# Cross attention with sixteen heads: the last key's share as a spread matmul and a VectorE product added to the diagonal blocks

## The reference, cut to what matters

```python
# x: 32 sequences of 32 queries, 512 wide; ctx_1024: 32 sequences of 257 keys, 512 wide
Q = (x_q @ W_Q + b_Q).reshape(B, L, H, dk).transpose(0, 2, 1, 3)
K = (x_k @ W_K + b_K).reshape(B, S, H, dk).transpose(0, 2, 1, 3)
V = (x_v @ W_V + b_V).reshape(B, S, H, dk).transpose(0, 2, 1, 3)
scores = jnp.einsum('bhld,bhsd->bhls', Q, K) / jnp.sqrt(jnp.float32(dk))
attn = jax.nn.softmax(scores, axis=-1)
ctx = jnp.einsum('bhls,bhsd->bhld', attn, V)
ctx = ctx.transpose(0, 2, 1, 3).reshape(B, L, H * dk)
out = ctx @ W_O + b_O
```

## Time and profile before

| what | us |
|---|---|
| median of 3 runs | 2437.06 |
| lowest and highest of them | 2435.38 and 2444.72 |
| the profiled execution | 2455.45 |
| its span in the trace | 2453.7 |
| set-up block of `cross_heads`, from its first matmul | about 971 to 1003 |
| its main block | about 1003 to 1611 |

### The profile page before, as it was taken

How to read it: one execution, slowest core, us unless ns; L and a number is a source line. 1 busy time by engine, 2 the same in 40 slices (tenths; PEclk the granted TensorE clock), 3 DMA queues, 4 the chain that set the end, 5 groups by cost and what they waited for, 6 DMA issues and landing times. The chain is left out here.

```text
span 2453.7 us, 39271 instructions
## 1 busy us (share of the span) xinstructions
PE 2102.0 (86%) x14020; PEld 1784.9 (73%) x14020; DVE 1126.3 (46%) x2057; ACT 898.0 (37%) x1479; POOL 926.3 (38%) x638
## 2 busy tenths in 40 slices
PE   6895888837999973999999999977665999999994
PEld 5543777637999962688888888865544999999993
DVE  4245463765555537222223322348754445544543
ACT  2112121214666642233333333223222555555551
POOL 2002312105777763222222222213212666666654
PEclk9996999957999986999999999968876999999997
DMA  3482000016888874011100100010003566656653
GB/s 124 178 312 108 18 19 33 1 35 238 277 278 279 280 230 175 23 33 27 35 26 26 31 31 26 18 48 5 22 22 129 198 217 213 211 198 217 214 194 124
DMA packets 102452, 299.03 MB, mean 122 GB/s; under 512 B 10912, under 2 KB 27936, under 8 KB 102336
## 3 DMA queue, kind: packets, MB, share of 16 engines
q1 hardware_dynamic: 76928, 232.88, 28.3%
q0 software_dynamic: 11840, 38.81, 5.1%
q10 hardware_dynamic: 13600, 26.22, 2.9%
HBM read 265.10 MB, written 32.77 MB: 121 GB/s over the span
## 5 line engine op out<-in xcount | busy, mean ns | idle before, releaser
L134 PE MATMUL banks<-ra 128*128 128x256 f32 (+3 forms) x3004 | 983.6, 328 | 65.9 <-DVE x L1040 24.3
L135 PE MATMUL banks<-ra 128*128 128x256 f32 (+3 forms) x3004 | 968.9, 323 | 0.1
L136 PE MATMUL banks<-ra 128*128 128x256 f32 (+3 forms) x3004 | 965.1, 321 | 3.4 <-issue 3.1
L134 PEld LDWEIGHTS banks<-ra 128*128 128x128 f32 (+1 forms) x3004 | 578.9, 193 | 131.8 <-issue 50.4
L136 PEld LDWEIGHTS banks<-ra 128*128 128x128 f32 (+1 forms) x3004 | 578.7, 193 | 45.2 <-issue 1.3
L135 PEld LDWEIGHTS banks<-ra 128*128 128x128 f32 (+1 forms) x3004 | 580.0, 193 | 39.0 <-issue 3.1
L1475 POOL TENSOR_TENSOR ra<-fa,ra 128x1024 fp32r<-128x1024 f32 x187 | 446.3, 2387 | 237.3 <-ACT ra L1508 236.3
L1508 ACT ACTIVATE ra<-fa 128x1536 fp32r<-128x1536 f32 x190 | 281.5, 1482 | 85.4 <-DMA fa<-in_L_units 68.2
L1592 DVE TENSOR_TENSOR ra<-fa,ra 128x256 fp32r<-128x256 f32 x190 | 162.1, 853 | 92.0 <-ACT ra L1532 91.5
L332 POOL TENSOR_TENSOR ra<-fa,ra 128x2048 fp32r<-128x2048 f32 (+2 forms) x22 | 85.7, 3905 | 285.3 <-ACT ra L326 278.6
L1567 DVE TENSOR_TENSOR ra<-fa,ra 128x512 fp32r<-128x512 f32 x190 | 133.6, 703 | 115.8 <-ACT ra L1508 109.0
(11 more groups left out here) (219 smaller groups left out, 2505.3 us busy)
## 6 DMA issues: line engine op xcount, KB each, us to landing
fa<-in_L_units SPq DMA_DIRECT2D x190, 768.0 KB, 4.5
fa<-in_ctxT SPq DMA_DIRECT2D x64, 514.0 KB, 4.1
ea_y_scratch<-fa ACTq DMA_DIRECT2D x35, 512.0 KB
fa<-in_ctx SPq DMA_DIRECT2D x32, 512.0 KB, 5.3
eb_y_scratch<-fa ACTq DMA_DIRECT2D x15, 512.0 KB, 3.6
fa<-in_L_attn_w_qkvT SPq DMA_DIRECT2D x6, 1024.0 KB, 7.3
normed_scratch<-na SPq DMA_DIRECT2D x16, 256.0 KB, 2.1
x<-in_x SPq DMA_DIRECT2D x1, 2048.0 KB, 8.6
```

What stands on the lines that cost most here:

```text
L134: pe.matmul(psum, lh, rh, start=first, stop=False)
L135: pe.matmul(psum, lh, rl, start=False, stop=False)
L136: return pe.matmul(psum, ll, rh, start=False, stop=last)
```

## The change

The last key's share of the output leaves `p_v`. Its probabilities are spread over the 32 values of a head by one matmul, and multiplied by the last key's values.

- Set-up: the job `None` computes the values of the last key the other way round, with `W_V` as the weights (still in `staging[1]` in full fp32) and the 32 columns of `lastT` moving, in 16 matmuls. VectorE adds the bias in one instruction, and makes `diag` in another. The store to DRAM and its two waits are gone. GpSimd makes `spread`, 128 by 128 with ones in blocks of 32 by 32, and no longer clears `vl`.
- POOL, each sequence: a product of 128 elements, `diag` times the last column of `pr` (`p_last[u]`), behind the normalisation.
- PE, each sequence: the ninth transpose becomes a matmul of 128 by 128 by 128, `spread` by `p_last[u]`, into bank 0. The four matmuls over four rows are gone from `p_v`.
- DVE, each sequence: a new product (`o_last`) of bank 0 and the last key's values between the copy of the second transposed half and `tops`; the four copies into `ot` become four additions with `o_last`.
- ACT loses the small copy of line 1856, SP the load of line 1787 and the wait before it.

```diff
                         if job is None:
...
-                            for c in range(DC):
-                                for part in range(2):
-                                    ins = pe.matmul(banks[0:B, 7, :], lastT[:, c, :], wv[part][:, c, :].bitcast(F32),
-                                                    start=c + part == 0, stop=c == DC - 1 and part == 1)
+                            for i in range(DC):
+                                for c in range(DC):
+                                    ins = pe.matmul(banks[:, 7, i * B:(i + 1) * B], staging[1][:, c, i * P:(i + 1) * P],
+                                                    lastT[:, c, :], start=c == 0, stop=c == DC - 1)
...
                         pool.tensor_tensor(pr[u][:, :, 0:S], pr[u][:, :, 0:S],
                                            rinv[:, u, :].unsqueeze(2).to_broadcast([P, DC, S]),
                                            ALU.mult).then_inc(s_pn, 1)
+                        eng.wait_ge(s_pn, m + 1)
+
+                        eng.sem_inc(s_norm, 1)
+                        shape = [P, DC, NQ]
+                        pool.tensor_tensor(p_last[u], diag.unsqueeze(1).to_broadcast(shape),
+                                           pr[u][:, :, S - 1:S].to_broadcast(shape), ALU.mult).then_inc(s_pl, 1)
...
-                        eng.wait_ge(s_t, 3 * n + 3)
-                        act.activation(pt[0:DC, 2, 0:P], banks[0:DC, 0, 0:P], ACT.Copy).then_inc(s_ta, 1)
...
                         dve.tensor_copy(pt[:, 1, :], banks[:, T1, :]).then_inc(s_td, 1)
+
+                        eng.wait_ge(s_bc, n + 1)
+                        dve.tensor_tensor(o_last, banks[:, 0, 0:P].rearrange("p (c q) -> p c q", c=DC),
+                                          v_last[:, :, bass.ds(n, 1)].to_broadcast([P, DC, NQ]), ALU.mult).then_inc(s_ol1, 1)
                         if after:
                             tops(n + 1, (j + 1) % 2)
                             sums(n + 1, (j + 1) % 2)
 
                         eng.wait_ge(s_pv, n + 1 + LEAD)
+                        eng.wait_ge(s_ol1, n + 2)
...
-                            ins = dve.tensor_copy(ot[rows, :, NQ * j:NQ * j + NQ], o[rows, :, rows])
+                            ins = dve.tensor_tensor(ot[rows, :, NQ * j:NQ * j + NQ], o[rows, :, rows], o_last[rows], ALU.add)
...
-                            eng.wait_ge(s_ta, 2 * m)
+                            eng.wait_ge(s_ol1, m)
...
-                        pe.transpose(banks[0:DC, 0, 0:P], pr[u][:, :, S - 1], ident[:]).then_inc(s_t, 1)
+                        eng.wait_ge(s_pl, n + 1)
+                        pe.matmul(banks[:, 0, 0:P], spread, p_last[u].rearrange("p c q -> p (c q)"), start=True,
+                                  stop=True).then_inc(s_bc, 1)
...
-                        eng.wait_ge(s_vld[u], 32 * g + 16 * (j // 2 + 1))
                         for c in range(DC):
                             cols = slice(c * P, (c + 1) * P)
                             for k in range(2):
-                                pe.matmul(banks[:, T1, cols], v[u][:, k, cols], pt[:, k, cols], start=k == 0, stop=False)
-                            ins = pe.matmul(banks[:, T1, cols], vlast[u][0:DC, cols], pt[0:DC, 2, 0:P], start=False,
-                                            stop=True)
+                                ins = pe.matmul(banks[:, T1, cols], v[u][:, k, cols], pt[:, k, cols], start=k == 0,
+                                                stop=k == 1)
```

More of the change, by code:

```diff
@@ L1667, in cross_heads @@
             qt, bvb, bob = f.take(DC, T), f.take(D), f.take(D)
-            bqc, bkc = f.take(DC), f.take(DC)
+            bqc, bkc, bvc = f.take(DC), f.take(DC), f.take(DC)
+            own, spread, diag, v_last = f.take(4), f.take(P), f.take(NQ), f.take(DC, B)
             qg = [f.take(DC, NQ) for _ in range(2)]
@@ L1672, in cross_heads @@
             staging = [f.take(DC, D) for _ in range(3)]
-            lastT, vl = f.take(DC, B), f.take(DC, D)
+            lastT = f.take(DC, B)
             wk, wv, wo = ((r.take(DC, D), r.take(DC, D)) for _ in range(3))
@@ L1681, in cross_heads @@
             layer_norm("nd", ahead=((load, high, low), (0, 1, 2), (0,)))
-            s_b, s_mm, s_out, s_vl = sem("xb_biases"), sem("xb_product"), sem("xb_taken"), sem("xb_last_v")
-            s_zero = sem("xb_zeros")
+            s_b, s_mm, s_out = sem("xb_biases"), sem("xb_product"), sem("xb_taken")
+            s_zero, s_own = sem("xb_zeros"), sem("xb_own_heads")
             s_ld = [sem(f"xb_ctx{u}") for u in range(2)]
@@ L1696, in _ @@
                                      (bob, d["L1_xattn_b_O"].partition_broadcast(P)),
+                                     (bvc, d["L1_xattn_b_Vc"]),
                                      (lastT, d["ctxLastT"])):
@@ L1703, in _ @@
                         eng.dma_start(stg[u][:, :, 0:S], d["ctxT"][u]).then_inc(s_ld[u], 16)
[L1704 to L1708, removed]
+                    eng.wait_ge(s_b, 96)
                 @block.gpsimd
                 def _(eng):
-                    pool.memset(vl[0:B], 0.0)
                     for u in range(2):
@@ L1715, in _ @@
                     ins.then_inc(s_zero, 1)
+                    pool.memset(own, 1.0).then_inc(s_own, 1)
+                    eng.wait_ge(s_own, 1)
+                    pool.affine_select(out=own, in_=own, compare_op=ALU.is_ge, fill=0.0, base=0,
+                                       pattern=[[-XD, 4]], channel_multiplier=1).then_inc(s_own, 1)
+                    eng.wait_ge(s_own, 2)
+                    pool.affine_select(out=own, in_=own, compare_op=ALU.is_gt, fill=0.0, base=XD,
+                                       pattern=[[XD, 4]], channel_multiplier=-1).then_inc(s_own, 1)
+                    eng.wait_ge(s_own, 3)
+                    pool.tensor_copy(spread.rearrange("p (h v) -> p h v", h=4), own.unsqueeze(2).to_broadcast([P, 4, XD]))
                     low(eng, (1, 2, 3))
@@ L1724, in _ @@
                 def _(eng):
-                    eng.wait_ge(s_b, 80)
+                    eng.wait_ge(s_b, 96)
                     for j, job in enumerate(jobs):
@@ L1728, in _ @@
                         if job is None:
-                            eng.wait_ge(s_zero, 1)
-                            for c in range(DC):
-                                cols = slice(c * P, (c + 1) * P)
-                                ins = dve.tensor_tensor(vl[0:B, c, cols], banks[0:B, 7, cols], bvb[0:B, cols], ALU.add)
+                            dve.reduce_sum(diag, ident[:].rearrange("p (h q) -> p q h", h=4), AX_X)
+                            ins = dve.tensor_tensor(v_last, banks[:, 7, 0:DC * B].rearrange("p (c b) -> p c b", c=DC),
+                                                    bvc.unsqueeze(2).to_broadcast([P, DC, B]), ALU.add)
                         else:
@@ L1763, in cross_heads @@
             v = [f.take(2, D) for _ in range(2)]
-            vlast = [f.take(D) for _ in range(2)]
+            p_last = [f.take(DC, NQ) for _ in range(2)]
+            o_last = f.take(DC, NQ)
             pr = [f.take(DC, SE) for _ in range(2)]
-            pt, ot = f.take(3, D), f.take(DC, P)
+            pt, ot = f.take(2, D), f.take(DC, P)
             mx, bias, rs, rinv = (f.take(2, DC) for _ in range(4))
@@ L1769, in cross_heads @@
             oh, ol = r.take(DC, P), r.take(DC, P)
-            s_vld = [sem(f"xb_vlast{u}") for u in range(2)]
+            s_norm, s_pl, s_bc, s_ol1 = (sem(f"xb_{n}") for n in ("normed", "p_last", "p_last_spread", "o_last"))
             (s_ch, s_cl, s_kp, s_vp, s_k, s_v, s_qb, s_sc, s_bias, s_ex, s_rinv, s_pn, s_t, s_ta, s_td, s_pv,
@@ L1783, in _ @@
                 def _(eng):
[L1784 to L1790, removed]
                     with eng.Fori(0, B // 2 - 1) as i:
@@ L1796, in _ @@
                             eng.dma_start(stg[u][:, :, 0:S], d["ctxT"][n]).then_inc(s_ld[u], 16)
-                            load_last(n, u)
                 @block.gpsimd
@@ L1872, in tile_out @@
                         act.activation(oh, ot, ACT.Copy).then_inc(s_oh, 1)
-                    eng.sem_inc(s_ta, LEAD)
+                    eng.sem_inc(s_ta, 1)
                     ctx_high(0, 0, 0)
@@ L1919, in step @@
                         eng.wait_ge(s_pv, n + 1 + LEAD)
+                        eng.wait_ge(s_ol1, n + 2)
+                        eng.sem_inc(s_passed, 1)
                         o = chunks(banks[:, T1, :])
@@ L1935, in _ @@
                     eng.sem_inc(s_o, 1)
+                    eng.sem_inc(s_ol1, 1)
                     keep_v(0, 0)
@@ L1999, in turn @@
                         eng.wait_ge(s_pn, n + 1)
-                        eng.wait_ge(s_ta, 2 * n + 1)
+                        eng.wait_ge(s_ta, n + 1)
                         eng.wait_ge(s_x, g + 1)
@@ L2117, in layouts @@
         "L1_xattn_b_Vi": i["L1_xattn_b_V"].reshape(DC, 4, XD).transpose(1, 0, 2).reshape(D),
```

(1 more changed line is left out.)

7 lines of the change are left out of this document (3 added, 4 removed).

## The result

The changed kernel takes 2370.91 us in the median of 4 runs (2365.08 to 2373.40), the kernel before 2438.03 on the same occasion. The ratio is 0.9706, with an interval from 0.9680 to 0.9733. By the medians that is 67 us less; by the ratio, which is estimated from the single runs and isn't the quotient of the two medians, 72 (65 to 78). 2368.2 had been forecast.

What follows compares the result with a forecast made beforehand. PE's issue was taken to bound the kernel. Terms -70.8 (`p_v`), -3.8 (last step), +9.1 (tile ends) and -3.4 (set-up) gave -68.9 us; off the median 2437.06 that is 2368.2, range 2352 to 2392 (8 in 10).

Steps and rivals of the forecast that it cites:

- What bounds the kernel: Main block of the layer: PE busy 569 of 580 us; edits elsewhere count only where they make PE wait.
- `p_v`: PE, each step: sixteen equal passes without row changes, 4.22 to 1.86 us, 2.36 less; 70.8 us over 30 steps.
- Spread matmul, `p_last`, `o_last`, additions: New work on PE, POOL and DVE each step: covered, 0 us; spread matmul at most 3 us in all.
- Tile ends: Third key group waits for `keep_k` behind DVE's later additions: 1.3 us at each of 7 tile ends, +9.1 us (6 to 13).
- S: The start of `p_v`, from which the times at a tile's end are counted.
- Last step: Layer's last step, `p_v` at half the clock with nothing hiding it: 7.5 us becomes 3.7, a gain of 3.8 us.
- step 30: Step before the last `turn`, where PE already waits 1.50 us on POOL: its gain from the shorter `p_v` is lost.
- Set-up: Job `None`: 32 passes with 32 columns take 3.6 us instead of 7.0, -3.4 us (bounds -4.5 and -1).
- the change of rows wasn't the reason: Rival for `p_v`: each chunk's first pass stays at 0.21 us, a step gains 1.64, total 2385.7 us; chance 0.15.
- The clock didn't fall at the tile ends: Answers the rival that PE's clock falls there, losing 2 us at each of 7, 2382 us in all; chance 0.10.
- The slower rival: `o_last` on DVE is long (about 3.5 us cancels the gain; at 4 us, 2453) and delays every step; chance 0.02.
- the tile ends wait less: Rival: additions and `oh` follow faster than worked out, less or no wait, down to 2359 us; chance 0.09.

Runs made afterwards that it cites:

- e_nolast: The kernel before without the last key's four matmuls in `p_v`, the old set-up and load kept: 2389.82 us, ratio 0.9719 to the kernel before.

## Why the prediction was right, point by point

The forecast was 68.9 us less. The medians of three comparisons gave 67.1, 73.1 and 74.9, the layer in the trace 73.7. So the mechanism was right and the size about 5 us too small; that the first pair of medians came within 2 us of the forecast is partly luck.

- **What bounds the kernel:** PE's issue. Right. Every experiment that shortened `p_v` shortened the step by as much, and only waits of PE, and more work on it, added anything.
- **`p_v`:** forecast -2.36 us a step, measured 4.22 - 1.81 = -2.41. The mechanism, a loss at each change between 128 and 4 rows, was chosen over a plain count of the four matmuls (1.64), and two variants of the kernel before show it: the same work in another order, 1.2 us gained; more rows, 1.55 us gained. The loss was sized wrongly in words: "about 0.1 us" for each change would make 24 x 0.11 + 8 x 0.1 = 3.4 us of `p_v`, and it took 4.22. A change costs 0.2. The gain wasn't hurt, since it was worked out as the measured 4.22 less sixteen passes.
- **What the sum missed:** in the loop `p_v` also starts some 0.1 us earlier. So a step gains 2.50 on average, and 30 of them 74.9 (65.2 measured, and 9.7 lost at the tile ends) in place of 70.8. This is the larger part of the 5 us by which the layer did better. The rows point to the wait for `vlast` that is gone. Before, two instructions of PE's sequencer stood between the end of DVE's copy (1255.61) and `p_v` (1255.94), the second (line 2019) for that wait; after, there is one (line 2030). `e_nolast` keeps both, and its `p_v` starts as late as before (2.09 to 2.11 us behind the first transpose); outside the loop, where no value is worked out, it starts at 1.86 in all three. No run takes out that wait alone.

```profile
L2018 PEldq ALU_OP  x1: 32/32/32, 1255.8 to 1255.8; - x1
L2019 PEldq FUSED_REGOPS  x1: 37/37/37, 1255.8 to 1255.8; - x1
```
- **Spread matmul, `p_last`, `o_last`, additions:** forecast 0 by themselves. Right: without them the 30 steps take the same time. POOL's product took 0.41 us in the median (0.4 had been estimated), but 0.74 at the seven tile ends, which is still covered; DVE's took 0.28 (0.29). One reason was wrong: `tops` moved by 0.11 us as forecast (0.13), but not because of `o_last`. It starts 0.90 us behind the first score matmul in both kernels, and the scores start 0.12 us later behind the spread matmul; `o_last` had made room for it before that.
- **Tile ends:** forecast +9.1 us, 1.3 each. The wait came where it was said, by the chain that was said, and nowhere else: `keep_k` at S + 5.53 (5.50 forecast), PE again at S + 6.04 (6.05). At the end shown PE loses 1.25 us in the gap, and 0.1 more because the first matmul behind it takes 0.22 us in place of 0.12. Taking the cause away gave back 9.7 us (484.9 - 475.2), 1.4 each.
- **Last step:** forecast -3.8 us. From the last but one `turn` to the next layer it was 26.4 and is 21.0, so -5.4. The term was mis-sized. From the start of `p_v` to that of DVE's work on its result it was 7.57 us and is 3.26, so -4.3: the last six of the sixteen passes start 0.11 us apart and not 0.21, because the granted clock was back at 1.00 from 1518.8. Another 0.5 us is in the last `turn`: its eight transposes took 1.46 us to the next matmul and take 1.00, since the clock fell 0.8 us behind their start now and 0.4 us before. And 0.7 us is in `tile_out`, whose twelve matmuls ran at the lower clock to the eleventh before and to the seventh now (first to last start 4.80 and 4.09 us). The last two `turn`s stand 0.1 us further apart.

```profile
1514.51 1.21 PE L2016 MATMUL banks<-ident,fa 128*128 128x128 f32 x8 [3.85 <-POOL fa L1812]
1515.51 0.63 PE L2023 MATMUL banks<-fa 128*128 128x128 f32 x2
1516.55 3.08 PE L2034 MATMUL banks<-fa 128*128 128x128 f32 x16 [0.40 <-issue]
```

The wait for POOL in this step grew from 1.50 us to 3.85, by 2.35: the gain of step 30 was lost as forecast.
- **Set-up:** forecast -3.4, measured 36.0 - 32.6 = -3.4. Its 32 passes took 3.65 us.

Sum of what was measured: -65.2 for the 30 steps (74.9 less 9.7), -5.4 for the end, -3.4 for the set-up, +0.2 for the first step, together -73.7 when the parts aren't rounded.

**The rivals.** That the change of rows wasn't the reason is refuted by two experiments. The clock didn't fall at the tile ends (1.00 from 1022 to 1508 us); why it fell after a 1.50 us gap in the last step before and not after these, no run tells. The slower rival put 1.0 us of slack behind `o_last`; at least 0.38 of it is there, and `o_last` itself, at 0.28 us, needs none. That the tile ends wait less is refuted by the seven waits of PE (7.9 us in all).

## What to carry to other kernels

Look at the starts of consecutive matmuls, not at their count: here four matmuls over few rows between others over many cost 2.4 us, where their eight passes, started 0.11 us apart, would be 0.9; the same work grouped by rows was faster, and so was a variant padded to full rows. When an engine that bounds the kernel gets faster at one place, follow the chain that it meets next with its new arrival time; here an engine's written order (`sums` before the additions) had been free and began to cost 1.4 us at each tile end. Look too at what the engine that bounds the kernel does between its own waits: a wait that comes last of several should need nothing worked out behind it. Compare the stage that changed within two traces rather than two profiled totals, which here differed by 17 us elsewhere.

## What the runs showed of the hardware that wasn't expected

- Twelve fp32 matmuls over 128 rows took 2.67 us, and eight over 128 rows with four over 4 rows between them 4.22. In the grouped order they took 3.04. Away from a change, passes over 4 and over 128 rows both start 0.11 us apart; each change between them cost 0.2 us, half ahead of it and half behind.
- Products of 128 columns on DVE take 0.28 us each but start 0.20 us apart when they follow each other, so one more costs 0.20.
- The order of three waits ahead of a matmul was worth 0.12 us a step in the loop, though all three had to be met either way: one register instruction of 0.03 us, behind the wait that was met last, held the matmul back by some 0.1 us.
- The 16 gathers of another layer, first start to last, took 41.4 to 41.9 us in the six traces of two chips and 56.1 to 57.2 in the four of a third, with variants of both kernels on either side. The runs don't tell why.
